# The first attention's last output projection moved into the feed-forward's stage, the experts' first weights and half of their norm made in the second attention's last steps, and the router computed with experts as rows

## What is computed

```
x = x + attention(layernorm(x))     # 16 heads of 16, window of 128, output @ w_o.T
x = x + ffn(layernorm(x))           # 4-bit weights with scales and LoRA, 256 -> 1024 -> 256, relu
x = x + state_space(layernorm(x))   # scan over 256 steps, 16 states
# last block, on y = layernorm(x)
z = y + attention(rmsnorm(y))       # 32 heads of 128, 4 key heads, causal, output @ Wo
t = rmsnorm(z) * ln2_w
router_scores = sigmoid(t @ Wr)     # 32 experts, best 8 of (score + bias), weights sum to 1
moe = sum_e w[:, e] * ((silu(t @ Wg[e]) * (t @ Wu[e])) @ Wd[e])   # all 32 are computed
x = x + z + moe + shared expert     # the shared one has the same shape
```

## Time and profile before

| | us |
|---|---|
| median of 3 runs | 1131.04 (1130.98 to 1133.48) |
| the profiled execution | 1135.74 |
| its span | 1133.9 |
| TensorE busy | 1040.5 |
| VectorE, ScalarE, GpSimd busy | 796.6, 689.7, 650.4 |

### The profile page before, as it was taken

How to read it: one execution, slowest core, us unless ns; L and a number is a source line. 1 busy time by engine, 2 the same in 40 slices (tenths; PEclk the granted TensorE clock), 3 DMA queues, 4 the chain that set the end, 5 groups by cost and what they waited for, 6 DMA issues and landing times. The chain is left out here.

```text
span 1133.9 us, 21387 instructions
## 1 busy us (share of the span) xinstructions
PE 1040.5 (92%) x6931; PEld 908.1 (80%) x6931; DVE 796.6 (70%) x1860; ACT 689.7 (61%) x1963; POOL 650.4 (57%) x688
## 2 busy tenths in 40 slices
PE   3799997986999679999999999999979999999998
PEld 3678776874555479999999999999968888888887
DVE  6667775556888678888888888888865555555555
ACT  2556563336999478888888788777833433433432
POOL 5344322543777478776877777666634455555553
PEclk9889997996999789999999999999978999999999
DMA  8000001002223020110001000000011111111111
GB/s 257 1 1 1 2 19 17 1 1 95 94 78 117 12 70 16 47 38 2 18 31 38 2 1 2 1 1 1 1 44 42 43 42 55 42 45 52 42 50 42
DMA packets 44083, 41.59 MB, mean 37 GB/s; under 512 B 6160, under 2 KB 40048, under 8 KB 44000
## 3 DMA queue, kind: packets, MB, share of 16 engines
q1 hardware_dynamic: 42384, 39.54, 11.4%
q10 hardware_dynamic: 1616, 0.99, 0.3%
HBM read 39.40 MB, written 1.11 MB: 36 GB/s over the span
## 5 line engine op out<-in xcount | busy, mean ns | idle before, releaser
L1880 POOL TENSOR_TENSOR prob<-prob,rden 128x128 f32<-128x128 f32 (+1 forms) x256 | 127.8, 521 | 83.7 <-DVE rden L1961 82.0
L2249 POOL TENSOR_TENSOR hid_l<-hid,hid_h 128x512 fp32r<-128x512 f32 x66 | 85.6, 1297 | 134.9 <-ACT hid_h L2218 134.9
L2276 DVE TENSOR_TENSOR hid<-psum,silu 128x512 f32<-128x512 f32 x66 | 45.6, 691 | 126.3 <-ACT silu L2216 126.3
L2216 ACT ACTIVATE silu<-psum 128x512 f32<-128x512 f32 x66 | 39.4, 598 | 117.9 <-PE psum L75 117.9
L2268 DVE SCALAR_TENSOR_TENSOR x<-psum,weight,x 128x256 f32<-128x256 f32 x264 | 108.8, 475 | 0.0
L73 PE MATMUL psum<-xt_h,gu_l 128*128 128x512 f32 x264 | 106.8, 404 | 0.3 <-DVE xt_l L167 0.3
L75 PE MATMUL psum<-xt_h,gu_h 128*128 128x512 f32 x264 | 105.4, 399 | 0.0
L1826 ACT ACTIVATE prob<-psum,neg_max 128x128 f32<-128x128 f32 (+1 forms) x256 | 105.1, 421 | 0.3
L74 PE MATMUL psum<-xt_l,gu_h 128*128 128x512 f32 x264 | 105.0, 398 | 0.0
L1345 POOL TENSOR_TENSOR drive<-u,b_all 128x1024 f32<-128x1024 f32 x32 | 75.7, 2366 | 42.3 <-DVE h L1464 20.6
L1863 POOL TENSOR_TENSOR qr<-r_part_a,r_part_b 128x512 f32<-128x512 f32 x64 | 82.8, 1294 | 6.5 <-DVE r_part_b L1918 6.5
(11 more groups left out here) (282 smaller groups left out, 3746.2 us busy)
## 6 DMA issues: line engine op xcount, KB each, us to landing
b_all<-scan_b_rows SPq DMA_DIRECT2D x16, 512.0 KB, 3.7
early<-in_L_ffn_Wq_dram SPq DMA_DIRECT2D x4, 1024.0 KB, 5.8
early<-in_L_ffn_Wo_dram SPq DMA_DIRECT2D x4, 1024.0 KB, 6.3
raw<-in_L_ffn_Wg_dram SPq DMA_DIRECT2D x32, 128.0 KB, 2.2
raw<-in_L_ffn_Wu_dram SPq DMA_DIRECT2D x32, 128.0 KB, 2.3
raw<-in_L_ffn_Wd_dram SPq DMA_DIRECT2D x32, 128.0 KB, 2.3
x<-_attn_hidden_states_dram SPq DMA_DIRECT2D x8, 128.0 KB, 4.9
early<-in_L_ffn_w_up_q_dram SPq DMA_DIRECT2D x1, 1024.0 KB, 7.4
```

The costliest lines, as they stand in the source:

```text
L1880: ins = pool.tensor_tensor(at, at, rden[:, s % 4, i:i + 1].to_broadcast([P, (i + 1) * P]), ALU.mult)
L2249: pool.tensor_tensor(hid_l[:, j, cols], hid[:, c, :], f(hid_h[:, j, cols]), ALU.subtract)\
```

## The change

- The last batch's turn and output product leave the first attention. A class `OutputProjection` holds their tensors and semaphores, and the feed-forward does the same instructions: turn first, the product behind up product 0, the sum behind VectorE's first plain copy. The norm of tiles 6 and 7 comes after it.
- In the feed-forward the bias transfers go from ScalarE to SP; ScalarE's normalised tiles come before activation 4 (before: 2), the copy of the down weights before 5 (before: 2), the high parts of the turned half before 6 (before: 5).
- A class `ExpertsEntry` holds the experts' first tensors. The raw weights lie in a buffer of the feed-forward that is free. They are loaded in the causal attention; gate and up weights of expert 0 and the router's weights are split there, and the norm of tiles 0 to 3 is made in the steps from 30 to 35 of the last group.
- The router's products have the router's weights as stationary operand: 12 matmuls of 512 columns onto 32 rows, six after each half of expert 0. The logits are copied and turned back by 8 turns in expert 1.
- In `experts`, the norm of tiles 4 to 7 follows, and the eight sums of `x` and `z` are spread.

```diff
-        self.vars_before, self.norms_before = core.norm_vars, core.norms
-        core.norm_vars, core.norms = core.norm_vars + len(self.rounds), core.norms + 1
+        if enter:
+            self.enter()
...
+    def enter(self):
+        self.vars_before, self.norms_before = self.c.norm_vars, self.c.norms
+        self.c.norm_vars, self.c.norms = self.c.norm_vars + len(self.rounds), self.c.norms + 1
...
-    def moments(self, dve, x, h):
-        for t in range(h * TH, (h + 1) * TH):
+    def moments(self, dve, x, h, tiles=None):
+        for t in tiles or range(h * TH, (h + 1) * TH):
...
+    def product(self, pe, b, n):
+        pe.wait_ge(self.lo, b + 1)
+        for t in range(2):
+            for k in range(KD):
+                ins = product(pe, self.core.psum[:, n, t * D:(t + 1) * D],
+                              self.core.xt(k, slice(b * S + t * P, b * S + (t + 1) * P)),
+                              (self.wo_h[:, k, :], self.wo_l[:, k, :]), k == 0 and t == 0, k == KD - 1, True)
+        ins.then_inc(self.done, 1)
+
+    def add(self, dve, b, n):
+        dve.wait_ge(self.done, b + 1)
+        at = self.core.x[:, 2 * b:2 * b + 2, :]
+        dve.tensor_tensor(at, self.core.psum[:, n, :].rearrange("p (t n) -> p t n", t=2), at, ALU.add).then_inc(self.x_added, 1)
...
             yield "normalise", 2 * B - 1
-            yield "turn_o", B - 1
-            yield "project_out", B - 1
...
+                for to, given in ((bias_up, b_up.rearrange("(k p) -> p k", p=P)),
+                                  (bias_down, b_down.rearrange("(a n) -> a n", a=1).to_broadcast([P, D]))):
+                    with nc.allow_non_contiguous_dma(reason="a bias of 1024 numbers"):
+                        sp.dma_start(to[:], given).then_inc(loaded_b, 16)
...
-                for to, given in ((bias_down, b_down.rearrange("(a n) -> a n", a=1).to_broadcast([P, D])),
-                                  (bias_up, b_up.rearrange("(k p) -> p k", p=P))):
-                    with nc.allow_non_contiguous_dma(reason="a bias of 1024 numbers"):
-                        act.dma_start(to[:], given).then_inc(loaded_b, 16)
                 act.wait_ge(ffn.summed, 8)
-                for at in UP:
+                for n, at in enumerate(UP):
                     act.activation(up_h[:, :, at], up_s[:, :, at], ACT.Copy).then_inc(w_hi, 1)
+                    if n == 0:
+                        output.high(act, LAST, OUTB[0])
                 act.wait_ge(loaded_b, 16 * 2)
                 for n in range(2 * KF):
                     m = n % KF
-                    if n == 2:
+                    if n == 5:
                         act.activation(down_h[:], down_s, ACT.Copy).then_inc(w_hi, 1)
+                    if n == 4:
                         act.wait_ge(shifted, 1)
                         for t in range(TH, NT):
                             act.activation(norm.y[:, t, :], core.x[:, t, :], ACT.Identity, bias=shift[:, t - TH:t - TH + 1],
                                            scale=norm.rs[:, t:t + 1]).then_inc(norm.normed, 1)
-                    if n == 5:
+                    if n == 6:
...
+                    if n == 0:
+                        output.low(dve, LAST, OUTB[0])
+                dve.wait_ge(output.x_added, LAST)
+                norm.moments(dve, core.x, 1, range(TH, NT - 2))
...
                     if n == 0:
+                        output.add(dve, LAST, OUTB[1])
+                        dve.wait_ge(output.x_added, LAST + 1)
+                        norm.moments(dve, core.x, 1, range(NT - 2, NT))
+                        norm.variance(dve, 1)
+                    if n == 2:
                         dve.wait_ge(norm.rstd_ready, norm.vars_before + 2)
                         dve.scalar_tensor_tensor(shift[:], norm.mv[:, TH:NT, 0], -1.0, norm.rs[:, TH:NT], ALU.mult,
                                                  ALU.mult).then_inc(shifted, 1)
-                    if n in (3, 6):
-                        down_low(n // 6)
+                    if n in (6, 8):
+                        down_low(n // 8)
...
+                output.turn(pe, LAST, OUTB[0])
                 norm.ready(pe, 0)
                 for n in range(KF):
                     up(n)
+                    if n == 0:
+                        output.product(pe, LAST, OUTB[1])
...
+        free = core.early[:, 3, :]
+        size = 2 * 3 * KD * FI
+        self.raw = free[:, 0:size].rearrange("p (j n c) -> p j n c", j=2, n=3)
...
+    def high(self, act, e, j):
+        act.wait_ge(self.loaded[j], 24 * e + (48 - 24 * j))
+        act.activation(self.gu_h[:, j], self.raw[:, j, 0:2, :].rearrange("p a (k n) -> p a k n", k=KD),
+                       ACT.Copy).then_inc(self.gu_hi, 1)
+
+    def low(self, pool, e, j):
+        pool.wait_ge(self.gu_hi, e + 1)
+        pool.tensor_tensor(self.gu_l[:, j], self.raw[:, j, 0:2, :].rearrange("p a (k n) -> p a k n", k=KD),
+                           f(self.gu_h[:, j]), ALU.subtract).then_inc(self.gu_ready, 1)
...
+                if last and n == STEPS + 2:
+                    yield "next_turn",
...
+                if last and n == STEPS + 2:
+                    yield "next_low", 0
+                if last and n == STEPS + 3:
+                    yield "next_low", 1
...
+                if last and n in (STEPS - 2, STEPS - 1):
+                    yield "next_moments", n - (STEPS - 2)
+                if last and n == STEPS - 1:
+                    yield "next_variance",
+                if last and n == STEPS:
+                    yield "next_split",
+                    yield "next_normalise",
...
+                entry.load_constants(sp)
+                for j in range(2):
+                    entry.load(sp, j, j)
...
+                def next_normalise():
+                    act.wait_ge(nxt.rstd_ready, nxt.vars_before + 1)
+                    for t in range(TH):
+                        act.activation(nxt.y[:, t, :], z[:, t, :], ACT.Copy, scale=nxt.rs[:, t:t + 1]).then_inc(nxt.normed, 1)
+
+                def next_turn():
+                    act.wait_ge(entry.loaded_c, 16 * 3)
+                    nxt.scalar(act, (0,))
...
+                def next_moments(n):
+                    if n == 0:
+                        nxt.begin(dve)
+                        dve.wait_ge(z_added, B * KVH1 + B - 1)
+                    nxt.moments(dve, z, 0, ((0, 1, 4, 5), (2, 3))[n])
+
+                def next_variance():
+                    nxt.variance(dve, 0)
+
+                def next_low(k):
+                    if k == 0:
+                        dve.wait_ge(entry.loaded_c, 16 * 3)
+                    nxt.low(dve, 0, (k,))
...
+                        if isinstance(e, int) and e == 0:
+                            if c == 0:
+                                norm.scalar(act, (1,))
+                            copy_logits(c)
...
-                norm.vector(dve, z)
+                def residual(t):
+                    dve.tensor_tensor(core.x[:, t, :], core.x[:, t, :], z[:, t, :], ALU.add).then_inc(added, 1)
+
+                norm.begin(dve)
                 own = norm.count
-                for t in range(NT):
-                    dve.tensor_tensor(core.x[:, t, :], core.x[:, t, :], z[:, t, :], ALU.add).then_inc(added, 1)
+                norm.moments(dve, z, 1, (6, 7))
+                norm.variance(dve, 1)
+                for t in range(2):
+                    residual(t)
+                norm.normalise(dve, z, 1)
+                for t in range(2, 4):
+                    residual(t)
+                norm.low(dve, 1)
...
-                norm.tensor(pe)
-
-                def route():
-                    pe.wait_ge(wr_ready, 1)
+                def router_products(c):
+                    if c == 0:
+                        pe.wait_ge(entry.wr_ready, 2)
+                    for k in range(KD):
+                        ins = product(pe, psum[0:NE, ROUTEB[c], :], (wr_h[:, k, :], wr_l[:, k, :]),
+                                      core.xt(k, slice(c * HALF, (c + 1) * HALF)), k == 0, k == KD - 1)
+                    ins.then_inc(routed, 1)
+
+                def turn_logits():
+                    pe.wait_ge(logits_out, 2)
                     for t in range(NT):
-                        for k in range(KD):
-                            ins = product(pe, psum[:, LOGITB, t * NE:(t + 1) * NE], core.xt(k, slice(t * P, (t + 1) * P)),
-                                          (wr_h[:, k, :], wr_l[:, k, :]), k == 0, k == KD - 1)
-                    ins.then_inc(logits, 1)
+                        ins = pe.transpose(psum[:, LOGITB, t * NE:(t + 1) * NE], logits_t[:, t * P:(t + 1) * P],
+                                           core.ident[0:NE, 0:NE])
...
+                            if isinstance(e, int) and e == 1 and c == 0 and n == 1:
+                                turn_logits()
...
+                        if isinstance(e, int) and e == 0:
+                            router_products(c)
```

(26 more changed lines are left out.)

228 lines of the change are left out of this document (120 added, 108 removed).

## The result

| | before | after |
|---|---|---|
| median, 20 runs each | 1131.75 | 1121.99 |
| ratio | | 0.9916 (0.9897 to 0.9935) |
| profiled execution, its span | 1135.74, 1133.9 | 1128.49, 1126.7 |
| TensorE busy | 1040.5 | 1033.1 |

The change makes the kernel faster by 9.5 us (7.4 to 11.7, the ratio times 1131.75). I forecast 14.0 less. The runs of the changed kernel lie in groups: 11 of 20 at 1119.04 to 1122.4 with a mean granted clock of 0.970 to 0.973, five at 1127.05 to 1128.89 with 0.962 to 0.967. Two more, of 1168.86 and 1279.03 at clocks of 0.835 and 0.743, are slow runs: they count in the table's median, which without them is 1121.24, but not in the ratio. The profiled execution is of the second group. That matters for how its trace is read.

The account below looks back on a forecast made before the run. TensorE, busy for 92% of the span, was the bound, so time could be won only where it waits or works slowly or needlessly. Savings of 5.0 + 9.0 = 14.0 took the median from 1131.04 to 1117.0, range 1113 to 1122.

Parts of the forecast that it names:

- Seam one: Windowed attention's end into the feed-forward: down product 0 starts at 206.5 instead of 211.56, 5.0 saved.
- Product 8: Ninth up product of the feed-forward: starts at 201.9 instead of 208.66, 6.8 earlier.
- The price in the attention: Causal attention's last steps: the added norm makes ScalarE wait for the power; the stage ends 2.8 later.
- The forecast's chain: Causal attention's tail: VectorE's aggregates end near 823.3, power near 824.3, ScalarE's probability copies start near 826.4 instead of 823.28.
- The entry: Causal attention's end to expert 2: expert 2 at 854.9 instead of 863.87, 9.0 saved with the tail's 2.8 paid.
- the first rival: No slow spell at the experts' entry: expert 0's first half takes 2.8, not 5.2; 1114.5, chance 0.18.
- the second: Clock falls again in the hole or before down product 0: 2.5 more each time, 1119.5 to 1122; chance 0.20.
- the row of 845.31 to 848.24: Old router's profile row: TensorE, though busy all the time, can lose its clock when its work is light.
- the hole: Normed tiles' turns and wait before expert 0's second half: about 3 us without ordinary matmuls, 838.3 to 841.3.
- Three things make it: Gain up to expert 2: norm leaves the path (-9.2), router costs less (-4.6), router no longer lowers clock (-2.8).
- The steps from expert 2 on, which I hold to be untouched: Experts' 31 remaining steps from expert 2 on are TensorE's alone, and the change leaves them as they are.
- The same saving gives 1117.0: Whole kernel: the 14.0 saved from the profiled 1135.74 also comes off the median before, 1131.04.

Follow-up runs that it names:

- down_low_early: Changed kernel with VectorE's second low part of the down weights one place earlier, ahead of plain copy 8; median 1118.94, ratio 0.9901 to the kernel before.
- norm_later: Changed kernel with ScalarE's four normalised tiles behind its copies of the last probabilities, and their turns later; median 1121.16, ratio 0.9907 to the kernel before.
- tail_no_norm: Changed kernel with the norm of tiles 0 to 3 back in the experts' stage, weights still split in the attention; median 1128.30, ratio 0.9958 to before.
- router_turned: Kernel before with seam one's change and the router turned around, experts' norm, weights and transfers as before; median 1122.96, ratio 0.9912 to before.
- seam1_only: Kernel before with seam one of the change alone, causal attention and experts as before; median 1127.62, ratio 0.9934 to the kernel before.
- seam2_only: Kernel before with only the causal attention's and experts' part of the change, feed-forward as before; median 1126.06, ratio 0.9936 to the kernel before.
- The second measurement: The changed kernel measured again with no edit; median 1120.06, ratio 0.9893 (0.9844 to 0.9943) to the kernel before.

## Why the prediction was half right

*Seam one, 5.0: right.* 24.1 in the mean of four profiles against 28.85, so 4.7. Product 8 came 7.0 sooner (forecast 6.8); product 0 took 5.4 after it (forecast 4.6), because VectorE's second low part starts late and takes 1.62, not 1.21. down_low_early shows that this low part is the wait: one place earlier, the stretch is 1.0 to 1.7 shorter.

*The price in the attention, 2.8: right in mechanism, too large.* ScalarE waits for the power (0.70), its copies of the last probabilities come 2.4 later (12.2 after the last but one sum into `z`, 9.9 before; I had 3.1), VectorE's low part waits 2.64 for them. Between the last two sums it costs 2.1, in every profile that has the norm there except norm_later's (1.6), and nothing in tail_no_norm. The whole stretch pays 618.35 - 616.48 = 1.9 in the means of four, but it also varies for reasons ahead of the tail. The forecast's chain has a slip besides: its own terms give 823.7 for the end of the aggregates, not 823.3.

*The entry, 11.8 between the attention's end and expert 2: the sum right, its terms not.* I had 23.5 and it is 23.6. But the first half of expert 0 runs at 2.4 GHz (2.87 for twelve matmuls, forecast 5.2), and the second behind the wait at 0.62 (4.46, forecast 2.8). So the first rival and the second both came, and cancelled, which is luck: 2.3 less in the first half, 1.7 more in the second and 0.7 more between them. Filled, the wait has no spell behind it: the row of 845.31 to 848.24, by which I held the hole harmless, was the wrong one to go by. The Trainium skill ("TensorE: Matmul & The Clock Gate", Part 4, PE-mode transpose) has turns not counting as busy in the way matmuls do; in seven of nine traces turns and a wait are followed by a slow spell, and no run tells the two apart. The old base is the other half: I took the 35.3 of one execution, and the four give 31.2 to 35.3, mean 34.0. The gain is 10.4 in the mean.

*"Three things make it": failed as an account.* I had the norm at 9.2, the router at 4.6 and the clock at 2.8 as separate terms. They aren't: with the router old the norm's move gives from nothing to 2.4, since TensorE's wait of nine and a half is partly replaced by a slow expert 0 (8.0 for its two halves, 7.2 before), by the norm's turns and wait between them (4.5) and by the tail's 2.1. The router's form alone is worth 31.49 - 23.6 = 7.9 in the changed kernel, as much as the 7.4 I had for it and the clock together (from one profile, with the long spell); what is left for the norm and the weights, with the tail, is 4.3 (router_turned) and not 6.4.

*"The steps from expert 2 on, which I hold to be untouched": wrong.* From expert 2 to the last wait of 0.56 or 0.57 before the end's down products it takes 264.2 in the kernel before, in seam1_only and in router_turned, and 265.05 in the changed kernel, seam2_only and tail_no_norm. The last two rows of that kind, of router_turned (expert 2 at 850.54) and of tail_no_norm (854.29):

```profile
1114.76 0.38 PE L73 MATMUL psum<-wd_h,hid_l 128*128 128x256 f32 x1 [0.57 <-POOL hid_l L2299]
```

```profile
1119.34 0.39 PE L73 MATMUL psum<-wd_h,hid_l 128*128 128x256 f32 x1 [0.56 <-POOL hid_l L2357]
```

That is 0.8 lost in matmuls with experts' gate and up weights, with no wait. It follows the tensors' new places or the program's form; which of these wasn't tried. The span's last piece, behind that last wait, is 5.8 to 5.9 in the kernel before and 6.1 to 6.4 in the changed one, another 0.4 in the landing of the last output.

*"The same saving gives 1117.0": this is the step that failed.* The forecast's 5.0 + 11.8 - 2.8 = 14.0 became, in the means of four profiles each, 4.7 + 10.4 - 1.9 = 13.2. The steps behind expert 2, which stood at nothing in it, take 0.8 of that and the end 0.4, which leaves 12.0, or 1119.0 on 1131.04; the larger group of runs is at 1119 to 1122. The median is above it since a third of the compared runs (6 of 18) are at 1127 or more, with a lower mean clock, as the profiled executions with the long slow spell are; that those runs have that spell is inferred from their clock, and not seen. I carried a saving read in one execution over to a median without asking how far executions of one kernel differ: those of before reach from 1128.21 to 1140.76. Nothing in the forecast stood for that, though the clock's spells in that execution could be read. The largest term of the sum, the entry, was mis-sized by it: 11.8 from one execution, 10.4 from four. Whether the long spell is more frequent with seam one (4 of 12 profiles against none of 5) stays open, as the kernel before has long runs too.

The second measurement, 0.9893, is 12.1 less (6.5 to 17.7), near the stretches' sum; 14.0 lies outside the interval of the first and inside that of the second.

## What to carry to other kernels

A slow spell that lies on a wait costs nothing, and the same spell on work moved there does: cost the entry with its spells before and after as one whole, not norm, router and clock each for itself. Matmuls of few columns are worth turning around: with the router turned, both its own time and the fall of the clock in it were gone (7.9 us in the changed kernel, by one profile). Half of this change, seam one with the router turned, measured as well as the whole (0.9912 against 0.9916): try the simple part alone first. Take several profiles of the kernel before, and compare stretches between fixed instructions: they told 1 us apart where medians could not tell 3.

## What was not expected of the hardware

- Unchanged work differs by 8 to 10 us between executions with the clock's slow spells (first attention's end 179.53 to 189.82), at places that are nearly the same each time: in 12 of 17 profiles a slow spell begins between 64.3 and 66.8, and it lasts from 3.4 to 24 us.
- Nine matmuls more made a stretch 1.5 shorter.
- Half steps of the experts, 24 matmuls each of the same shapes at the same clock and with no wait, took 4.240 instead of 4.227 (mean of 61, from start to start) in every kernel with `ExpertsEntry`; the 0.013 lies in the gate and up products.
